# First attention of a two-layer graph network: ScalarE scales the keys and values of its last two steps, and edge columns and counts move in the order

## The reference

```python
edge_index = jnp.stack([src, dst])
xn = _layernorm(x, axis=-1)
x = x + _L0_gnn_ref(xn, ..., edge_index) + _L0_mix_ref(xn[None], ...)[0]
...
def _L0_mix_ref(x, w_map, g_k, b_k, g_v, b_v, w_out, b_out):
    qkv = x @ w_map.T
    q, k, v = jnp.split(qkv, 3, axis=-1)        # 12 heads of 64
    k = _layernorm(k, g_k, b_k)                 # over each head's 64 columns
    v = _layernorm(v, g_v, b_v)
    attn = jnp.einsum('bhnd,bhne->bhde', k, v) / n
    out = jnp.einsum('bhnd,bhde->bhne', q, attn)
    return out @ w_out.T + b_out
```

## Time and profile before

| what | value |
|---|---|
| time, median of 3 runs | 1956.26 us (1954.53 to 1958.17) |
| the profiled execution's own time | 1956.79 us |
| its span | 1954.8 us |
| TensorE busy | 1847.9 us (95%) |
| VectorE busy | 1292.1 us (66%) |
| ScalarE busy | 935.6 us (48%) |
| granted TensorE clock, mean | 0.973 |

### The profile page before, as it was taken

How to read it: one execution, slowest core, us unless ns; L and a number is a source line. 1 busy time by engine, 2 the same in 40 slices (tenths; PEclk the granted TensorE clock), 3 DMA queues, 4 the chain that set the end, 5 groups by cost and what they waited for, 6 DMA issues and landing times.

```text
span 1954.8 us, 30891 instructions
## 1 busy us (share of the span) xinstructions
PE 1847.9 (95%) x12157; PEld 1753.5 (90%) x12158; DVE 1292.1 (66%) x2489; ACT 935.6 (48%) x1547; POOL 151.3 (8%) x127
## 2 busy tenths in 40 slices
PE   6997999999999999888789999999999999999998
PEld 5875789998899998788689999999999999999998
DVE  6997766555246566778857653456666666676886
ACT  2331223425124546779533233345555566666775
POOL 1000000003000023333100000000101001001010
PEclk9997999999999999889799999999999999999999
DMA  3110002101113103010132132265657557677795
GB/s 118 50 49 1 25 25 106 57 12 64 49 49 113 66 28 111 1 39 17 65 124 74 50 105 73 73 222 193 221 182 232 206 209 253 223 256 246 285 326 195
DMA packets 36844, 234.30 MB, mean 120 GB/s; under 512 B 5964, under 2 KB 7366, under 8 KB 14680
## 3 DMA queue, kind: packets, MB, share of 16 engines
q1 hardware_dynamic: 31366, 217.41, 31.4%
q0 software_dynamic: 2656, 8.99, 2.1%
q10 hardware_dynamic: 2674, 5.87, 0.8%
HBM read 221.91 MB, written 10.35 MB: 119 GB/s over the span
## 4 chain that ended last, share of the span: by engine, by line
PE 44%; issue 3%; DVE 3%; ACT 1%; DMA 1%; POOL 0%; ACTq 0%; POOLq 0%; DVEq 0%
PE bank L2755 8%; PE bank L341 7%; PE bank L342 7%; PE bank L343 7%; PE bank L2756 4%; PE bank L2767 3%; PE bank L2771 2%; PE bank L2759 2%; PE bank L2768 2%; PE bank L2770 1%; PE bank L2758 1%; DVE weight_lo L314 1%; PE bank L2713 0%; DMA weight_raw_fifth<-in_ffn_w 0%; DMA out<-ffn_y,slot_token 0%
## 5 line engine op out<-in xcount | busy, mean ns | idle before, releaser
L314 DVE TENSOR_TENSOR weight_lo<-weight_raw,weight_hi 128x2304 fp32r<-128x2304 f32 (+1 forms) x155 | 391.9, 2533 | 52.0 <-ACT weight_hi L304 51.9
L304 ACT ACTIVATE weight_hi<-weight_raw 128x2304 fp32r<-128x2304 f32 (+1 forms) x155 | 323.3, 2087 | 67.1 <-DMA weight_raw<-in_ffn_w 46.5
L341 PE MATMUL bank<-xT_hi,weight_hi 128*128 128x320 f32 (+1 forms) x576 | 184.0, 319 | 5.3 <-DVE xT_lo L362 5.2
L342 PE MATMUL bank<-xT_lo,weight_hi 128*128 128x320 f32 (+1 forms) x576 | 179.0, 311 | 0.0
L343 PE MATMUL bank<-xT_hi,weight_lo 128*128 128x320 f32 (+1 forms) x576 | 178.9, 311 | 0.0
L341 PE MATMUL bank<-weight_hi,xT_hi 128*128 128x384 f32 (+1 forms) x480 | 161.4, 336 | 9.6 <-DVE weight_lo L314 6.2
L3135 DVE TENSOR_TENSOR hidden_tmp<-hidden_tmp,bank 128x160 f32<-128x160 f32 (+5 forms) x192 | 65.5, 341 | 158.3 <-ACT hidden_tmp L2918 157.4
L342 PE MATMUL bank<-weight_lo,xT_hi 128*128 128x384 f32 (+1 forms) x480 | 157.4, 328 | 0.0
L343 PE MATMUL bank<-weight_hi,xT_lo 128*128 128x384 f32 (+1 forms) x480 | 157.3, 328 | 0.0
L613 PE MATMUL bank<-one_hot_dst,one_hot_src 125*128 125x313 f16 x800 | 123.7, 306 | 15.2 <-ACT packed_counts L627 7.9
L2918 ACT ACTIVATE hidden_tmp<-bank,ffn_b_by_load 128x160 f32<-128x160 f32 (+5 forms) x192 | 73.7, 404 | 119.5 <-PE bank L2759 112.8
(11 more groups left out here) (495 smaller groups left out, 5030.1 us busy)
## 6 DMA issues: line engine op xcount, KB each, us to landing
weight_raw<-in_ffn_w SPq DMA_DIRECT2D x111, 1152.0 KB, 5.2
weight_raw_fifth<-in_ffn_w SPq DMA_DIRECT2D x25, 1152.0 KB, 5.2
weight_raw<-in_shared_w SPq DMA_DIRECT2D x16, 1152.0 KB, 5.0
weight_raw<-in_mix_kv SPq DMA_DIRECT2D x8, 1152.0 KB, 5.1
weight_raw<-in_gat_w SPq DMA_DIRECT2D x8, 768.0 KB, 4.1
weight_raw<-in_mix_q SPq DMA_DIRECT2D x4, 1152.0 KB, 5.1
weight_raw<-in_mix_out SPq DMA_DIRECT2D x4, 1152.0 KB
weight_raw<-in_gnn_w SPq DMA_DIRECT2D x4, 1152.0 KB, 5.1
```

Source lines behind the costliest of these rows:

```text
L304: act.activation(upper_, whole_, ACT.Copy).then_inc(*w_hi.one())
L314: dve.tensor_tensor(lower_, whole_, upper_.bitcast(F32), ALU.subtract).then_inc(*w_lo.one())
L341: pe.matmul(dst, a[0], b[0], start=first, stop=False)
L342: pe.matmul(dst, a[0], b[1], start=False, stop=False)
```

## The change

In steps 2 and 3 (`SCALED_BY_SCALAR`) VectorE no longer multiplies the five tiles by the reciprocal. ScalarE does it, head by head, in six instructions of 128x64 for each tile (`scaled`), each with a column of `kv_stats` as its scale. VectorE's second loop (the gain) waits for them tile by tile. Two things move: one edge column of VectorE goes from behind `weights_lo` to behind the third subtraction, and in ScalarE's step 3 the copies of the counts go from behind `query(0, 0)` to the place between the second square and the third. `acts_until` only counts ScalarE's instructions for the semaphores.

```diff
+        SCALED_BY_SCALAR = (2, 3)
+
+        def acts_until(n):
+            return sum(6 + (TT if i in SCALED_BY_SCALAR else 0) for i in range(n))
...
                 for t in range(TT):
+                    if n == 3 and t == 2:
+                        edges_scalar(STEP[0])
                     act.wait_ge(*kv_ready.at(n * 2 * TT + t + 1))
                     act.activation(squares[:, n % KV, 6 * t:6 * t + 6, :], kv[:, r, t, :].rearrange("p (h d) -> p h d", d=DH), ACT.Square).then_inc(*acted.one())
                 following(n, 0)
-                act.wait_ge(*sums_ready.at(n + 1))
+                act.wait_ge(*sums_ready.at(2 * n + 1))
                 act.activation(kv_stats[:, 1, :], kv_stats[:, 1, :], ACT.Sqrt).then_inc(*acted.one())
-                for i in range(1, TT):
-                    following(n, i)
+                for i in range(TT):
+                    if i > 0:
+                        following(n, i)
+                    if n in SCALED_BY_SCALAR:
+                        scaled(n, i)
                 act.wait_ge(*kv_ready.at((n + 1) * 2 * TT))
                 upper(at(kvp, ALL, n % KV, ALL, ALL), kv[:, r, :, :]).then_inc(*kv_hi.one())
+
+            def scaled(n, t):
+                act.wait_ge(*sums_ready.at(2 * n + 2))
+                for h in range(6):
+                    head = kv[:, n % 2, t, h * DH:(h + 1) * DH]
+                    end = act.activation(head, head, ACT.Copy, scale=kv_stats[:, 2, 6 * t + h:6 * t + h + 1])
+                end.then_inc(*acted.one())
 
             def following(n, i):
...
-                edges_scalar(STEP[i])
+                if n < 3 or i > 0:
+                    edges_scalar(STEP[i])
...
                 for t in range(TT):
                     dve.tensor_tensor(z[t], z[t], wide(n6(0, t)), ALU.subtract).then_inc(*kv_ready.one())
-                    edges_vector(1 if t < STEP[0] - 2 else 0)
+                    edges_vector(1 if t < STEP[0] - 1 else 0)
                 weights_lo(c0 + n)
-                edges_vector(1)
                 if n > 0:
                     lower_halves(n - 1)
                 edges_vector(1)
...
                 for step in range(3):
...
                     for t in range(TT):
...
+                        if n in SCALED_BY_SCALAR and step == 0:
+                            edges_vector(1 if t < STEP[2] else 0)
+                            continue
+                        if n in SCALED_BY_SCALAR and step == 1:
+                            dve.wait_ge(*acted.at(acts_until(n) + 6 + t + 1))
                         dve.tensor_tensor(z[t], z[t], o, ALU.add if step == 2 else ALU.mult).then_inc(*made.one())
```

More of the change, by code:

```diff
@@ L859, in keys_or_values @@
                 edges_vector(1)
-                dve.wait_ge(*acted.at(6 * n + TT))
+                dve.wait_ge(*acted.at(acts_until(n) + TT))
                 own_step(dve.tensor_reduce(kv_stats[:, 1, :], squares[:, n % KV, :, :], AX_X, ALU.add))
@@ L865, in keys_or_values @@
                     query(0, 0)
-                dve.wait_ge(*acted.at(6 * n + 6))
-                dve.reciprocal(kv_stats[:, 2, :], kv_stats[:, 1, :]).then_inc(*dve_own.one())
+                dve.wait_ge(*acted.at(acts_until(n) + 6))
+                dve.reciprocal(kv_stats[:, 2, :], kv_stats[:, 1, :]).then_inc(*sums_ready.one())
                 dve.wait_ge(*kv_ready.now())
                 for step in range(3):
-                    dve.wait_ge(*dve_own.now())
+                    if step == 0:
+                        dve.wait_ge(*sums_ready.at(2 * n + 2))
+                    else:
+                        dve.wait_ge(*dve_own.now())
                     for t in range(TT):
```

## The result

The changed kernel takes **1959.78 us** (median of 20 runs, 1957.31 to 1965.02), the kernel before 1955.98 us (20 runs, 1951.5 to 1958.17). The ratio is 1.0023, with a 95% interval of 1.0016 to 1.0029: slower by 3.8 us, which is about the 0.2% that the prediction calls the limit of what can be told; the interval of the 20 runs lies above 1. The profiled execution took 1960.32 us, its span is 1958.5 us.

The account below looks back on a forecast made before the run. TensorE bounds the kernel, but from about 136 us VectorE's chain sets group 1's start. 8.0 us late, less 2.35 of multiplies and 2.85 of waits, gives +2.8: 1959.6 from the profile, 1959.1 from the median; 1959.5 taken, range 1956 to 1966.

Parts of the forecast that it names:

- VectorE's new wait: VectorE's gain loop in step 2, before the last tile: a new wait of about 6.9 us for ScalarE's scaling.
- Six scalings: ScalarE's six 128x64 instructions for one tile: 1.6 us, bounds 1.2 and 2.1 us.
- Tile 4: VectorE's gain multiply of step 2's last tile starts at 144.2 instead of 136.25, 8.0 us late.
- TensorE's advance: TensorE around 115 to 127 us, through the moved edge column: 0.3 us gained, 1.7 us as upper end.
- The waits near 120: TensorE's 3.60 us wait for a column near 115 becomes two shorter ones at 119 and 122.
- Counts: ScalarE's copies of the counts start at 153.1 instead of 152.58; TensorE's 7.31 us wait grows by 0.5 us.
- Step 3: VectorE's chain to `lower_halves`: 2.35 us of multiplies and 2.85 us of waits for TensorE go; it ends 2.8 us later.
- Group 1: TensorE's start of per_head's second group, behind `lower_halves`: at 187.1 instead of 184.34.
- At the same clock after it: Behind the start of per_head's group 1 all engines work as before at the same clock; the rest moves as a whole.
- B: Rival: clock stays low through per_head's group 0, adding 3.4 to 4.5 us; 1964 to 1966 us, chance 0.30.
- C: Rival: clock doesn't fall at 186 us, saving 4.9 us, end at -2.1 us; 1954.5 us, chance 0.12.
- D: Rival: ScalarE's scaling never late, counts copied about 7 us earlier; -5.7 us, 1950.8 us, chance 0.06.

Follow-up runs that it names:

- the first experiment: Against the changed kernel, step 2's tiles 3 and 4 scaled right behind tile 2, ahead of step 3's copies; 1954.5 us, ratio 0.9989 to the kernel before.
- 2 (weight behind) and 3: Against the changed kernel, the weight's upper part on ScalarE put behind the scaling of step 2's last tile; 1957.55 us, ratio 1.0014 to the kernel before.
- that of 1958.51 us: A repeat execution of the kernel with ScalarE scaling only in step 3, counts' copies moved, edge column unmoved; 1958.51 us, that kernel's median 1955.14 us.

## Why the prediction was right

**The sum, step by step.** *VectorE's new wait:* 6.9 us said, 6.63 us measured; the 1.42 us before tile 3 were called "a little late", without a number. *Six scalings:* 1.6 us said, 1.53 us measured, with bounds of 1.2 and 2.1. The price came from an instruction ten times as wide and held. (The lower bound should be 1.0 by its own 0.095 us less for each.) *Tile 4:* 8.0 us late said, 144.81 against 136.25, so 8.6 us measured. The 0.6 us are TensorE's advance: I took 0.3 us ahead, it was 0.33 us behind. This is the one term of the sum with the wrong sign. The waits near 120 did split as said, 2.05 us ahead of 121.25 and 1.36 us ahead of 124.09, but the low clock moved later with them and slowed the first head matmuls. *Counts:* copies at 153.1 said, 153.58 measured; the wait 0.5 us longer said, 0.67 us measured. *Step 3:* both waits for TensorE vanish, as said; from tile 4 to the start of `lower_halves` it is 185.31 - 144.81 = 40.50 us, before 182.13 - 136.25 = 45.88 us, so 5.38 us less, where 2.35 + 2.85 = 5.20 us were said. *Group 1:* 187.1 said, 187.52 measured. It is so 3.2 us later than before (184.34), and not 2.8. By 200 us TensorE has 0.5 us of this back, as its next wait there is 1.02 us where it was 1.52; the prediction had no such term. The mark is +2.7 us for a sum of +2.8: the path is the one foretold, the last tenths are luck.

**The total** was nearer than its parts deserve. The medians differ by 3.8 us, where the sum had 2.8; the profiled executions by 3.5 us. The microsecond between is from falls of the clock after 450 us, for which the prediction had no term. "At the same clock after it" is the one step that did not hold, by 1 us here and by up to 5 us in single executions. In the 20 runs the time goes with the clock: that of 1957.31 us has a mean clock of 0.975, those of 1964.17 and 1965.02 us have 0.971 and 0.969; a mean doesn't say where it fell. The upper end of the range, 1961.5, is not reached by the terms named for it, which end at 1959.6 + 0.5 + 0.3 = 1960.4; the measured 1959.78 lies inside either.

**The rivals.** *B* (low clock through all of group 0, 1964 to 1966 us) came about in part: the first seven matmuls of group 0 were slow, the rest at full clock, and the group lasted 132.29 - 126.49 = 5.80 us instead of 5.08. Of the 20 runs three are at or above 1964 us; none of these has a profile, and whether group 0 or the clock at 700 us makes them is open. The prediction called itself wrong if the clock at 124 to 132 or at 186 to 196 us differed from before. Both do: 0.75 against 0.98, and 0.67 against 0.50. (The first comes from the moved column: alone it gives 0.75 too.) It cost little, since only the first seven matmuls of group 0 were slow, and the low stretch of group 1 only came later: 0.50 was granted from 189.5 to 199.5 us. *C* (no fall at 186) did not come: the clock is 0.71 and 0.67 between 178 and 196 us, behind waits of TensorE of 2.02 us (ahead of 175.23) and 3.05 us (ahead of 187.52). By the rule of the Trainium skill in "TensorE: Matmul & The Clock Gate", "What's actually happening", waits this short should have kept the full clock; the trace still disagrees. *D* (ScalarE never late, -5.7 us) is the first experiment, where the mark came to -4.3 us: the mechanism holds, and the size was 1.4 us too large, within what profiles of one kernel differ by. (From 1956.8 its -5.7 us give 1951.1, not 1950.8.)

**What the parts are worth**, by the mark (differences are taken before rounding). The last column is the granted clock between 115 and 200 us in the same profiles (before: 0.82):

| scaling in step | counts | column | mark, us | less its offset | clock |
|---|---|---|---|---|---|
| none | - | moved | +0.4 | +0.2 | 0.82 |
| none | moved | - | -5.2 | -5.6 | 0.88 |
| none | moved | moved | -2.9 | -2.5 | 0.84 |
| 3 | moved | - | -6.7, -6.1, -4.4 | -7.0, -5.2, -4.2 | 0.88, 0.86, 0.84 |
| 3 | moved | moved | -4.5 | -4.2 | 0.86 |
| 2 (early) and 3 | moved | moved | -4.3 | -4.2 | 0.86 |
| 2 (weight behind) and 3 | moved | moved | +1.0 | +1.8 | 0.82 |
| 2 and 3 | moved | moved | +2.7, +1.7, +3.0 | +2.6, +2.6, +2.6 | 0.80, 0.82, 0.80 |
| 2 and 3 | - | - | +5.0 | +5.9 | 0.80 |

One kernel's profiles differ by up to 2.8 us less their offsets, so smaller steps prove nothing. Larger ones are the late scaling in step 2, which costs 6.8 us (-4.2 to +2.6), and the counts' move without the column's, which gains 5.6 us. That the column's move takes some 3 us of it back is what two single profiles suggest, but their clocks are 0.88 and 0.84, and for one and the same kernel that difference went with 2.8 us. Step 3's scaling gains some 1.5 us if profiles of equal clock are compared (-7.0 against -5.6 at 0.88, -4.2 against -2.5 at 0.84); that is an estimate from four profiles. The prediction had the first as 8.0 us late at tile 4, the second as copies that would start at 145.1 if VectorE were not late (measured 143.93 to 145.74), and saw that the one takes the other away.

**A version that beats both kernels** is likely, though not beyond doubt: the counts' move alone (ratio 0.9990, up to 0.9999) or tiles 3 and 4 scaled early (0.9989, up to 0.9998), 2 us each. Both intervals end just below 1, and eight kernels were compared. Of the 5.2 and 4.3 us at the mark about half is left in the medians. That a lead can go to the clock in later stages is shown in the profile of tiles 3 and 4 scaled early (nearly all of it, between 760 and 980 us) and in that of 1958.51 us; the counts' move has one profile, its fastest run, which keeps its lead, so for its median this is not shown.

## What to carry to other kernels

An operation given to an idler engine isn't done when its data is there, but when all that stands ahead of it in that engine's queue is: here 1.53 us of work came 6.6 us too late, behind a copy that waited for a third engine and a weight's upper part of 2.12 us. Put it in the queue by the time its input is ready, ahead of whatever waits for something later, and look at what the late result delays in turn. And move several things in several versions: of the three parts of this change the counts' move gave the gain, the column's gave nothing by itself, and the scaling in step 2 took it all back.

A window that starts after a wait can't show it. Look at the last wait ahead of a stretch, too, before calling what happens in it causeless; and look whether the same wait stands in the executions where nothing happened.

## What the runs showed of the hardware

- A ScalarE instruction over 128x64 with its scale from memory costs 1.53 us for six in a row, about 0.25 us each.
- TensorE's granted clock fell between 700 and 720 us in some executions (0.76 and 0.83) and not in others of the same program (1.00), though TensorE was busy for 20.00 of 20.00 us in that stretch in one of them. It cost 4.8 us there. The low clock began 0.7 us after TensorE had ended a wait of 0.74 us; eleven other profiles have the same wait and no fall, so what decides is open.
- Executions of one program spread over up to 16 us (1946.9 to 1962.5 us in twelve runs), while in three profiles of the changed kernel its stage came out alike to 0.1 us (in three of another kernel to 2.8 us, with a granted clock of 0.88, 0.86 and 0.84 in it). A gain of 5 us in a stage is then plain in a trace at a mark behind it, and hard to see in a few runs' times.
